# Reordering the steps ahead of the sort loop in a graph layer with residual and layer norm

## The chip, the cores and the metric

The kernel runs on one core of a Trainium2 chip. A core has a matrix engine (TensorE, in the profile PE, with its weight loads as PEld), a vector engine (VectorE, DVE), a scalar engine (ScalarE, ACT), a general engine (GpSimd, POOL) and a queue engine (SyncE, SP), which issues most of the transfers. Each runs its own list of instructions in order and waits for the others on semaphores. The metric is the device time of one execution in microseconds; the median of three runs is given.

## The reference

A node table x of 100,000 rows of 128 values, 50,000 edges with a source and a destination (ordered by destination), one weight matrix and a bias. Each edge sends the transformed row of its destination to its source; the sums are added to x and each row is normalised.

```python
row, col = (edge_index[0], edge_index[1])        # src, dst
messages = jnp.einsum('ei,oi->eo', x[col], W) + b
out = jax.ops.segment_sum(messages * agg_weight, row, num_segments=x.shape[0])
...
x = _layernorm(x + out, axis=-1)
```

## The kernel before, in words

The kernel first sorts the edges by source into a table and then walks over the nodes in 196 groups of 512. For every 4 groups (a period) there are 9 lists of up to 128 edges each; an edge's *bucket* is twice the number of its list, plus one if it lies in the last part of the list (its *tail*). Edges that a list can't hold spill into the next one.

**Decoding (DVE, lines 739 to 760).** The 50,000 sources lie in `src_rows` as 128 x 4 x 128. From them DVE makes the position in the span (`pos`), the list (`chunk`) and the bucket. The bucket's upper part (`e0`, up to 56 values) and lower part (`e1`, 16 values) are turned by PE (`turn_rows`, four 128x128 transposes each) so that edges lie along partitions, and DVE copies them to `hi_col` and `lo_col`. `hi_rows` goes to memory and comes back, spread over partitions, as `hi_row`.

**One-hots and totals (lines 764 to 770 and 539 to 545).** For each of 25 tile groups of 16 columns (2048 edges) DVE makes one-hots of both parts and PE adds up their products in one bank, 400 matmuls in all: the number of edges in each bucket.

**The rest of the way to the loop (lines 772 to 825).** DVE packs each edge into two words (`word1`, `word2`), copies sources and destinations as floats to `turn` (`chunk` is copied with the decoding), prepares constants (`ident_bf`, `not_earlier`, `part_half`), compares the first two row loads (`first_hots`), reads the totals (`counts`, `excess`), splits the bias in three parts (`b_parts` to `b3`), makes a running sum over the excess (`spill_row`) and from it the starting ranks (`origin`) and the largest list (`most_wide`). The excess goes through SP's queue into one row (`excess_row`), and the running sum back through it (`spilled`). PE turns the words and the float copies (lines 546 to 551), ScalarE copies them out (`s_cvt` counts, lines 1018 to 1021), and PE starts the loop when six copies are made.

**The sort loop (`count`/`place` on PE, `rank`/`spread` on DVE, `clip`/`second_word` on ScalarE).** For each tile group k PE counts ranks: products of one-hots, then a matmul that adds what came before (`carry`, for k = 0 from `origin`). DVE reads the ranks (`own`), and makes `slot`, `t_now` and `place_row`. Of the 16 columns of a group, 10 are placed by PE (`spread` makes the one-hots for it), and 6 by GpSimd, which scatters them to memory with indirect transfers (line 480), 141 in all. Work on k and the placing of k - 1 are interleaved by `lagging`.

**The overflow test.** In `rank(0)` DVE takes the largest list (turned by PE, `s_mxT`), sets the flag `over` and the factors `keep` and `dump` that make `place_row`. PE waits for the flag in group 1, since its ranks use the same bank.

**The main loop.** When all scatters have landed, SP loads the table back, DVE decodes it (36 columns first) and GpSimd gathers rows of x into `xg` by the table (line 517), a ring of 4 periods. Empty places in the table don't bring a row, so `xg` must hold no stray values at the start: GpSimd clears it (line 473) ahead of its first scatter. DVE, PE and ScalarE then make the sums, the projection and the norm of each group.

`after(...)` on DVE counts a semaphore up at an instruction's end and waits for it, so what follows doesn't overlap it:

```python
def after(ins):
    step_no[0] += 1
    ins.then_inc(s_bp, 1)
    dve.wait_ge(s_bp, step_no[0])
```

## Time and profile before

| | |
|---|---|
| median of three runs | 911.15 us (911.13 to 911.59) |
| the profiled execution | 912.28 us |
| its span, first to last instruction | 910.6 us |
| DVE busy | 853.0 us (94%) |
| PE busy / weight loads | 718.8 (79%) / 542.4 us (60%) |
| ScalarE busy | 650.4 us (71%) |
| GpSimd busy | 604.1 us (66%) |
| mean granted clock of PE | 0.931 |

The profile is one execution. Busy shares are averages over stages that differ: decoding and one-hots up to about 44 us, the sort loop up to about 247, the main loop from about 256 to the end. A row of a timeline gives the start, the length, the engine, the line and operation, output and inputs with sizes, how many such instructions were merged, and in brackets how long the engine was idle before it and who ended that. The granted clock is a share of TensorE's full 2.4 GHz: 1.00 or 0.50 (1.2 GHz).

### The profile page before, as it was taken

To read this page: it belongs to the slowest core of one execution; us is meant where nothing else is said; L and a number is where in the kernel's file an instruction comes from. 1 tells how busy PE (TensorE), PEld (TensorE's weight loads), DVE (VectorE), ACT (ScalarE), POOL (GpSimd) and SP (SyncE) were. 2 spreads that over 40 slices of the span, in tenths; PEclk is the share of its full clock that TensorE was granted. 3 is DMA by queue.
4 is the path that set the end of the run, shared out by engine and by line. 5 is a ranking of instruction groups with operands and counts; after the bars stand their busy time and mean duration, and the time that the engine had idled before them with its cause. 6 is when DMAs were issued, how large, how long until landed. Compare 5 with 4: busy or idle time off the path is not lost.

```text
span 910.6 us, 24246 instructions
## 1 busy us (share of the span) xinstructions
PE 718.8 (79%) x7748; PEld 542.4 (60%) x7773; DVE 853.0 (94%) x3868; ACT 650.4 (71%) x1683; POOL 604.1 (66%) x608
## 2 busy tenths in 40 slices
PE   3869999999638877777778877787878778787784
PEld 2835555555326656666666666676667667676664
DVE  7978999999658999999999999999999999999997
ACT  0147777777504778788778877777777887877788
POOL 3047777776657777777777777677777777777710
PEclk9969999999857999999999999989899999989988
DMA  2001111110043766676666667666666667666653
GB/s 73 2 26 37 39 41 39 43 37 26 16 134 108 209 212 214 220 215 215 206 212 212 208 211 212 205 209 211 208 220 207 205 214 215 208 214 202 217 176 124
DMA packets 81228, 141.20 MB, mean 155 GB/s; under 512 B 19552, under 2 KB 20588, under 8 KB 81100
## 3 DMA queue, kind: packets, MB, share of 16 engines
q1 hardware_dynamic: 62476, 110.55, 36.7%
q0 software_dynamic: 18624, 29.08, 13.3%
q8 instruction: 63, 1.03, 0.5%
q14 instruction: 65, 0.53, 0.2%
HBM read 87.64 MB, written 51.93 MB: 153 GB/s over the span
## 4 chain that ended last, share of the span: by engine, by line
DVE 61%; issue 7%; POOL 4%; ACT 1%; PE 1%; DMA 0%; ACTq 0%; DVEq 0%; POOLq 0%
DVE stats L994 16%; DVE h L988 10%; DVE sel L979 10%; DVE rest L977 8%; DVE xl L982 7%; DVE mv L1000 7%; POOL xg L517 3%; DVE rstd L1004 1%; ACT y L1087 1%; POOL place_scratch L480 1%; DVE shift L1008 1%; DVE now L965 1%; DMA xg<-in_x,now 0%; PE bank L719 0%; ACT aggT L1074 0%
## 5 line engine op out<-in xcount | busy, mean ns | idle before, releaser
L517 POOL DMA_INDIRECT xg<-in_x,now x441 | 449.0, 1018 | 172.9 <-issue 129.4
L1087 ACT ACTIVATE y<-h,shift,rstd 128x128 f32<-128x128 f32 x784 | 320.1, 479 | 0.1
L719 PE MATMUL bank<-wT,aggT 128*128 128x128 f32 x1568 | 241.5, 300 | 0.0
L719 PEld LDWEIGHTS bank<-wT,aggT 128*128 128x128 f32 x1568 | 202.6, 202 | 28.2 <-issue 11.9
L689 PE MATMUL bank<-sel,xg 128*128 128x308 bf16 (+11 forms) x685 | 171.1, 262 | 23.6 <-DVE xl L982 23.5
L480 POOL DMA_INDIRECT place_scratch<-word_col,place_row x141 | 142.1, 1008 | 55.6 <-issue 50.6
L691 PE MATMUL bank<-sel,rest 128*128 128x308 bf16 (+11 forms) x685 | 177.2, 262 | 0.0
L994 DVE BATCH_NORM_STATS2 stats<-h 128x6 f32<-128x128 f32 x784 | 169.5, 278 | 0.2
L693 PE MATMUL bank<-sel,xl 128*128 128x308 bf16 (+11 forms) x685 | 167.4, 261 | 0.0
L1081 ACT ACTIVATE std<-mv,eps 128x4 f32<-128x4 f32 x196 | 58.3, 298 | 132.7 <-DVE mv L1000 132.6
L988 DVE SCALAR_TENSOR_TENSOR h<-bank,aw,xt 128x512 f32<-128x512 f32 x196 | 145.6, 743 | 0.8 <-PE bank L719 0.4
L716 PE MATMUL bank<-b,deg 32*128 32x128 bf16 x784 | 39.1, 216 | 127.3 <-ACT aggT L1074 127.0
L1074 ACT COPY aggT<-bank 128x512 f32<-128x512 f32 x196 | 110.2, 562 | 30.9 <-PE bank L693 30.9
L979 DVE TENSOR_SCALAR sel<-iota_win,now 128x308 bf16<-128x308 f16 (+1 forms) x441 | 109.8, 296 | 0.0
L646 PE MATMUL bank<-oh_t,oh_s 128*128 128x441 bf16 x500 | 108.5, 355 | 1.6 <-ACT oh_s L1053 1.1
L716 PEld LDWEIGHTS bank<-b,deg 32*128 32x128 bf16 x784 | 24.4, 92 | 137.4 <-ACT aggT L1074 136.1
L977 DVE TENSOR_TENSOR rest<-xg 128x384 f32<-128x384 f32 x196 | 87.6, 447 | 12.3 <-DMA xg<-in_x,now 12.3
L689 PEld LDWEIGHTS bank<-sel,xg 128*128 128x128 bf16 x685 | 70.7, 103 | 35.3 <-issue 20.4
L1053 ACT ACTIVATE oh_s<-oh_s,ratio_col 128x128 bf16<-128x128 bf16 x250 | 83.9, 396 | 6.1 <-DVE oh_s L872 3.2
L982 DVE TENSOR_TENSOR xl<-rest 128x384 bf16<-128x384 f32 x196 | 88.1, 450 | 0.0
L874 DVE TENSOR_SCALAR oh_t<-iota_nb,t_now 128x441 bf16<-128x441 f16 x250 | 86.1, 344 | 0.0
L872 DVE TENSOR_SCALAR oh_s<-iota_nb,slot,word_col 128x128 bf16<-128x128 f16 x250 | 85.7, 343 | 0.0
(154 smaller groups left out, 927.1 us busy)
## 6 DMA issues: line engine op xcount, KB each, us to landing
xt<-in_x SPq DMA_DIRECT2D x195, 256.0 KB, 3.7
out<-y SPq DMA_DIRECT2D x195, 256.0 KB, 2.4
xg<-in_x,now POOLq DMA_INDIRECT x441
hi_row<-hi_scratch SPq DMA_DIRECT2D x50, 128.0 KB
place_scratch<-word_col,place_row POOLq DMA_INDIRECT x141
place_scratch<-scattered SPq DMA_DIRECT2D x1, 441.0 KB, 3.5
scattered<-place_scratch SPq DMA_DIRECT2D x1, 441.0 KB, 3.2
src_rows<-in_src SPq DMA_DIRECT2D x1, 192.0 KB
```

What stands on the lines that cost most here:

```text
L480: nc.gpsimd.indirect_dma_start(out=place_scratch, out_offset=bass.IndirectOffsetOnAxis(ap=place_row[:, k, i:i + 1], axis=0), in_=word_col[ ...
L517: nc.gpsimd.indirect_dma_start(out=xg[:, m, k], out_offset=None, in_=x, in_offset=bass.IndirectOffsetOnAxis(ap=now[:, m, k, 0:1], axis=0)) ...
L689: nc.tensor.matmul(AGG[q][:, nodes], top[:, ring, k, :, 1], sel[:, half, k, cols], start=(i == 0), stop=False, skip_group_check=True)
L691: nc.tensor.matmul(AGG[q][:, nodes], middle[:, half, k, :, 1], sel[:, half, k, cols], start=False, stop=False, skip_group_check=True)
L693: last = nc.tensor.matmul(AGG[q][:, nodes], xl[:, half, k], sel[:, half, k, cols], start=False, stop=(i == len(lists) - 1), skip_group_che ...
L719: last = nc.tensor.matmul(OUT[u % RO][:, nodes[j]], aggT[:, u % RO, nodes[j]], wT[:], start=False, stop=True, skip_group_check=True)
L977: V.tensor_tensor(rest[:, m % 2, lists], xg[:, m, lists], top[:, m, lists, :, 1], ALU.subtract).then_inc(s_upper, 1)
L979: V.tensor_scalar(sel[:, m % 2, k, 0:WIDTH[k]], iota_win[:, WIN[k]:WIN[k] + WIDTH[k]], now[:, m, k, 1:2], None, ALU.is_equal).then_inc(s_s ...
L982: V.tensor_tensor(xl[:, m % 2, lists], rest[:, m % 2, lists], middle[:, m % 2, lists, :, 1], ALU.subtract).then_inc(s_lower, 1)
L988: V.scalar_tensor_tensor(h[:, u].rearrange("p j d -> p (j d)"), OUT[u % RO][:], aw[:], xt[:, u].rearrange("p j d -> p (j d)"), ALU.mult, A ...
L994: V.bn_stats(stats[:, u, j], h[:, u, j]).then_inc(s_stats, 1)
L1087: nc.scalar.activation(y[:, u, j], h[:, u, j], ACT.Identity, bias=shift[:, u, j:j + 1], scale=rstd[:, u, j:j + 1]).then_inc(s_y, 1)
```

## The change

It touches the stretch between the first load and the sort loop, and one place in the loop's first group.

1. *Decoding.* The bucket is made in one piece: the whole position (`pos`, now with the upper bits) times 9, from which the upper part is one shift, and the lower part a mask, a shift-and-mask, a comparison and one two-input step that writes `turn[:, 2]` as floats. The upper part is copied for PE first, and PE waits for each part by itself. `hi_rows` has a semaphore of its own. `chunk` and its float copy move behind the totals.
2. *Totals.* `counts` and `excess` come right behind the one-hots, ahead of the words. The running sum comes ahead of `first_hots`.
3. *Transposes and copies.* PE and ScalarE take `word1` first, then `word2`, then `chunk`, sources, destinations; DVE's first ratio step waits for four copies, not six.
4. *Bias parts* come behind `most_wide`.
5. *Overflow test* in `rank(0)` comes behind `t_now`, ahead of `place_row`.
6. *xg* is cleared by ScalarE with one activation over 128 x 4608, ahead of its first copy, not by GpSimd.

```diff
@@ gpsimd
-            nc.gpsimd.memset(xg[:], 0.0).then_inc(s_clean, 1)
@@ tensor
-            pe.wait_ge(s_rows, 3)
+            pe.wait_ge(s_rows, 1)
             turn_rows(bank[1], turn[:, 1])
+            pe.wait_ge(s_rows, 2)
             turn_rows(bank[2], turn[:, 2])
...
-            pe.wait_ge(s_rows, 7)
+            pe.wait_ge(s_rows, 3)
+            turn_rows(bank[3], word1[:].bitcast(f32))
+            pe.wait_ge(s_rows, 4)
+            turn_rows(bank[2], word2[:].bitcast(f32))
             turn_rows(bank[0], turn[:, 0])
-            turn_rows(bank[3], word1[:].bitcast(f32))
-            turn_rows(bank[2], word2[:].bitcast(f32))
+            pe.wait_ge(s_rows, 6)
@@ vector, decoding
-            after(V.tensor_scalar(e1[:], src_rows[:], 2, P - 1, LSR, AND))
-            V.tensor_scalar(e2[:], src_rows[:], SPAN_N - GN, None, AND)
+            V.tensor_scalar(e1[:], src_rows[:], (1 << 18) - GN, None, AND)
+            after(V.tensor_scalar(e2[:], src_rows[:], 2, P - 1, LSR, AND))
             after(V.tensor_tensor(pos[:], e0[:], e1[:], OR))
-            after(V.tensor_tensor(e0[:], pos[:], e2[:], OR))
-            V.tensor_scalar(e2[:], src_rows[:], SPAN_BITS, None, LSR)
-            after(V.tensor_scalar(e0[:], e0[:], float(LISTS), None, ALU.mult))
-            V.tensor_scalar(e1[:], e0[:], SPAN_BITS, None, LSR)
-            after(V.tensor_scalar(e0[:], e0[:], SPAN_N - 1, None, AND))
-            after(V.scalar_tensor_tensor(chunk[:], e2[:], float(LISTS), e1[:], ALU.mult, ALU.add))
-            after(V.tensor_scalar(e0[:], e0[:], float(TAIL_FROM), None, ALU.is_ge))
-            after(V.scalar_tensor_tensor(bucket[:], chunk[:], 2.0, e0[:], ALU.mult, ALU.add))
-            V.tensor_scalar(e0[:], bucket[:], LO_BITS, None, LSR)
-            after(V.tensor_scalar(e1[:], bucket[:], LO - 1, None, AND))
-            V.tensor_copy(hi_rows[:], e0[:]).then_inc(s_rows, 1)
+            after(V.tensor_tensor(pos[:], pos[:], e2[:], OR))
+            after(V.tensor_scalar(bucket[:], pos[:], float(LISTS), None, ALU.mult))
+            after(V.tensor_scalar(e0[:], bucket[:], SPAN_BITS + LO_BITS - 1, None, LSR))
             V.tensor_copy(turn[:, 1], e0[:]).then_inc(s_rows, 1)
-            V.tensor_copy(turn[:, 2], e1[:]).then_inc(s_rows, 1)
-            V.tensor_copy(turn[:, 0], chunk[:]).then_inc(s_rows, 1)
+            V.tensor_scalar(e1[:], bucket[:], SPAN_N - 1, None, AND)
+            after(V.tensor_scalar(e2[:], bucket[:], SPAN_BITS, LO // 2 - 1, LSR, AND))
+            after(V.tensor_scalar(e1[:], e1[:], float(TAIL_FROM), None, ALU.is_ge))
+            V.scalar_tensor_tensor(turn[:, 2], e2[:], 2.0, e1[:], ALU.mult, ALU.add).then_inc(s_rows, 1)
+            V.tensor_copy(hi_rows[:], e0[:]).then_inc(s_hi_rows, 1)
+            dve.wait_ge(s_cols, 2)
+            V.tensor_copy(hi_col[:], bank[1][:]).then_inc(s_hilo, 1)
             dve.wait_ge(s_cols, 3)
-            V.tensor_copy(hi_col[:], bank[1][:]).then_inc(s_hilo, 1)
@@ scalar
+            act.wait_ge(s_made, 1)
+            nc.scalar.activation(xg[:].rearrange("p r k d -> p (r k) d"), ones[:].unsqueeze(1).broadcast_to([P, RX * LISTS, D]),
+                                 ACT.Copy, scale=0.0).then_inc(s_clean, 1)
```

What moves on DVE between the one-hots and the loop is shown by its order of instructions. DVE, from word2 on, before: the totals (`counts`, which wait for PE's 400 matmuls by `s_hist`) stand behind the copies, the constants and both row comparisons.

```order
L778 TENSOR_TENSOR word<-e 128x512 [waits s_bp]
L779 CAST turn<-src_rows 128x512
L780 CAST turn<-dst_rows 128x512
L781 CAST ident_bf<-ident 128x128
L782 TENSOR_SCALAR not_earlier<-later 128x512
L784 MEMSET spill_row 1x1
L786 TENSOR_SCALAR upper_half<-part 128x1
L787 TENSOR_TENSOR part_half<-part,upper_half 128x1 [waits s_bp]
L791 TENSOR_SCALAR oh_hiT<-hi_row,part_half 128x1024 [waits s_hrow0,s_bp]
L791 TENSOR_SCALAR oh_hiT<-hi_row,part_half 128x1024 [waits s_hrow1]
L797 TENSOR_TENSOR counts<-bank,guard 56x16 [waits s_hist]
L799 SCALAR_TENSOR_TENSOR excess<-counts 56x8 [waits s_bp]
```

The same engine in the changed kernel, right behind the last one-hot (L775 is the first step on `dst_rows`, L784 and L787 make `e0`, L785 makes `e1`):

```order
L775 TENSOR_SCALAR e<-dst_rows 128x512 [waits s_dst]
L776 TENSOR_SCALAR upper_half<-part 128x1
L778 TENSOR_TENSOR counts<-bank,guard 56x16 [waits s_hist]
L780 SCALAR_TENSOR_TENSOR excess<-counts 56x8 [waits s_bp]
L782 TENSOR_SCALAR word<-e 128x512
L783 TENSOR_SCALAR chunk<-bucket 128x512
L784 TENSOR_SCALAR e<-pos 128x512
L785 TENSOR_SCALAR e<-dst_rows 128x512
L786 CAST turn<-chunk 128x512 [waits s_bp]
L787 TENSOR_SCALAR e<-e 128x512
L788 TENSOR_TENSOR word<-e 128x512 [waits s_bp]
```

The totals have moved ahead of both words, so the words now stand behind the wait for PE.

PE in the changed kernel, from its last of the 400 matmuls (L542) to the first matmul of the sort loop (L597); before, all twenty transposes followed one wait for `s_rows`, with `chunk` first:

```order
L542 MATMUL bank4<-oh_lo,oh_hi 56x16 x15
L532 MATMUL bank3<-ident,word1 128x128 [waits s_rows]
L532 MATMUL bank3<-ident,word1 128x128 x3
L532 MATMUL bank2<-ident,word2 128x128 [waits s_rows]
L532 MATMUL bank2<-ident,word2 128x128 x3
L532 MATMUL bank0<-ident,turn 128x128 x4
L532 MATMUL bank6<-ident,turn 128x128 [waits s_rows]
L532 MATMUL bank6<-ident,turn 128x128 x3
L532 MATMUL bank1<-ident,turn 128x128 x4
L597 MATMUL bank6<-not_earlier,ident_bf 128x512 [waits s_hiT,s_cvt,s_zero]
```

The first four transposes can now start while DVE still makes word2; the loop's first matmul waits for the same six copies as before.

DVE in `rank(0)` of the changed kernel; before, L852 to L856 (the overflow test) stood ahead of `own`:

```order
L838 TENSOR_TENSOR own<-bank,oh_lo 128x256 [waits s_q,s_bp]
L842 TENSOR_REDUCE place_at<-own 128x16 [waits s_own]
L844 TENSOR_SCALAR beyond<-place_at 128x16 [waits s_place_at]
L846 SCALAR_TENSOR_TENSOR slot<-place_at,beyond 128x16 [waits s_beyond]
L848 SCALAR_TENSOR_TENSOR t_now<-beyond,t_col 128x16
L852 TENSOR_REDUCE most_all<-bank 128x1 [waits s_mxT]
L853 TENSOR_SCALAR over<-most_all 128x1 [waits s_bp]
L854 TENSOR_SCALAR keep<-most_all 128x1
L855 TENSOR_SCALAR most_all<-most_all 128x1
L856 TENSOR_SCALAR dump<-dump,most_all 128x400 [waits s_bp]
L859 SCALAR_TENSOR_TENSOR linear<-slot,t_now 128x16 [waits s_slot,s_bp]
L862 SCALAR_TENSOR_TENSOR place_row<-linear,keep,dump 128x16 [waits s_linear]
```

The five steps of the test now lie between the reading of the ranks and `place_row`.

## Rows read from the trace of the kernel before

**Rows 1.** The chain of waits at the sort's end: start us, length us, what.

```profile
247.20 8.37 issue
```

**Rows 2.** The page's groups: busy us, mean ns, idle us before and releaser.

```profile
L480 POOL DMA_INDIRECT place_scratch<-word_col,place_row x141 | 142.1, 1008 | 55.6 <-issue 50.6
```

**Rows 3.** Timeline of GpSimd, first scatter of tile groups 0, 1 and 2.

```profile
57.15 1.18 POOL L480 DMA_INDIRECT place_scratch<-word_col,place_row  x1 [7.66 <-issue]
...
67.12 0.96 POOL L480 DMA_INDIRECT place_scratch<-word_col,place_row  x1 [2.34 <-DVE place_row L864]
...
75.74 0.97 POOL L480 DMA_INDIRECT place_scratch<-word_col,place_row  x1 [0.89 <-DVE place_row L864]
```

**Rows 4.** Timeline of DVE from the totals to the first ranks.

```profile
40.20 0.16 DVE L797 TENSOR_TENSOR counts<-bank,guard 56x16 f32<-56x16 f32 x1
...
43.56 1.08 DVE L813 TENSOR_TENSOR_SCAN spill_row<-excess_row,zero_row 1x448 f32<-1x448 f32 x1
...
45.12 0.57 DVE L818 TENSOR_TENSOR ratio_col<-word_col,ratio_col 128x64 f32<-128x64 f32 x1
46.64 2.87 DVE L821 CAST origin<-spilled 56x8 bf16<-56x8 f32 x1 [0.95 <-DMA spilled<-spill_row]
...
49.78 0.28 DVE L825 TENSOR_SCALAR most_wide<-ones,most_hi 56x128 f32<-56x128 f32 x1
50.83 0.22 DVE L835 TENSOR_REDUCE most_all<-bank 128x1 f32<-128x56 f32 x1 [0.77 <-PE bank L624]
...
51.39 0.43 DVE L839 TENSOR_SCALAR dump<-dump,most_all 128x400 f32<-128x400 f32 x1
54.42 0.42 DVE L847 TENSOR_TENSOR own<-bank,oh_lo 128x256 bf16<-128x256 f32 x1 [2.60 <-PE bank L611]
```

**Rows 5.** Timeline of GpSimd ahead of its scatters.

```profile
43.98 1.08 POOL L470 CAST src_idx<-src_col 128x512 int32<-128x512 f32 x1 [35.72 <-ACT dst_col L1021]
...
45.55 3.93 POOL L473 MEMSET xg<- 128x4608 f32 x1
```

**Rows 6.** Timeline of PE: the totals, eight transposes, the origin matmul.

```profile
17.78 18.84 PE L542 MATMUL bank<-oh_lo,oh_hi 128*56 128x16 bf16 x400 [2.24 <-DVE oh_hi L770]
...
39.60 1.91 PE L533 MATMUL bank<-ident,word 128*128 128x128 f32 x8
...
49.59 0.32 PE L585 MATMUL bank<-origin,ident_bf 128*56 128x144 bf16 x1 [4.32 <-DVE origin L822]
```

**Rows 7.** Timeline of DVE during decoding.

```profile
7.38 0.69 DVE L744 TENSOR_TENSOR e<-pos,e 128x512 int32<-128x512 int32 x1
...
8.46 0.41 DVE L746 TENSOR_SCALAR e<-e 128x512 int32<-128x512 int32 x1
...
16.18 0.68 DVE L760 CAST lo_col<-bank 128x512 bf16<-128x512 f32 x1
```

**Rows 8.** Timeline of ScalarE, its first and its last copy before the loop.

```profile
9.27 0.27 ACT L1017 COPY wT<-bank 128x128 f32<-128x128 f32 x1 [7.17 <-PE bank L529]
...
43.25 0.58 ACT L1021 COPY dst_col<-bank 128x512 f32<-128x512 f32 x1 [0.27 <-PE bank L533]
```

**Rows 9.** Stretches: busy us of PE, PEld, DVE, ACT, POOL; granted clock, DMA share, GB/s.

```profile
36.70:44.00 7.30, 4.53 (x20) 4.22 (x22) 6.78 (x26) 3.00 (x5) 0.03 (x1) 1.00 0.00 0
46.70:49.60 2.90, 0.01 (x1) 0.01 (x1) 2.82 (x4) 0.00 (x0) 2.79 (x1) 0.60 0.54 180
49.60:54.40 4.80, 4.13 (x50) 2.49 (x52) 1.34 (x7) 2.61 (x6) 0.00 (x0) 0.50 0.02 4
```

**Rows 10.** Timeline of PE, the same work of tile groups 0 and 3.

```profile
51.20 1.01 PE L595 MATMUL bank<-not_earlier,ident_bf 128*128 128x512 bf16 x2
52.15 0.61 PE L601 MATMUL bank<-oh_hiT 64*128 64x128 bf16 x8
...
77.56 0.59 PE L595 MATMUL bank<-not_earlier,ident_bf 128*128 128x512 bf16 x2
78.08 0.40 PE L601 MATMUL bank<-oh_hiT 64*128 64x128 bf16 x8
```

More of the change, by code:

```diff
@@ L770, in _, with first_hots @@
                 V.tensor_tensor(oh_hi[:, k], pairs(hi_col, HI), digits(HI), ALU.is_equal).then_inc(s_ohk, 1)
+            def first_hots(k):
+                dve.wait_ge(s_hrow[k], 32)
+                V.tensor_scalar(oh_hiT[:, k], hi_row[:, k], part_half[:], None, ALU.is_equal).then_inc(s_hiT, 1)
             dve.wait_ge(s_dst, 48)
             V.tensor_scalar(e2[:], dst_rows[:], 4, 16, LSR, LSL)
-            after(V.tensor_scalar(e0[:], pos[:], 16, None, LSL))
-            V.tensor_scalar(word1[:], e2[:], FULL, None, OR)
-            V.tensor_scalar(e1[:], dst_rows[:], 15, 25, AND, LSL)
+            V.tensor_scalar(upper_half[:], part[:], 64.0, -64.0, ALU.is_ge, ALU.mult)
+            dve.wait_ge(s_hist, 1)
+            after(V.tensor_tensor(counts[:], SORT[0][0:HI, 0:LO], guard[:], ALU.add))
+            heads, tails = (counts[:].rearrange("h (c two) -> h c two", two=2)[:, :, i] for i in range(2))
+            V.scalar_tensor_tensor(excess[:], heads, -float(P), tails, ALU.add, ALU.add).then_inc(s_excess, 1)
+            V.tensor_scalar(word1[:], e2[:], FULL, None, OR).then_inc(s_rows, 1)
+            V.tensor_scalar(chunk[:], bucket[:], SPAN_BITS, None, LSR)
+            V.tensor_scalar(e0[:], pos[:], GN - 1, 16, AND, LSL)
+            after(V.tensor_scalar(e1[:], dst_rows[:], 15, 25, AND, LSL))
+            V.tensor_copy(turn[:, 0], chunk[:])
             after(V.tensor_scalar(e0[:], e0[:], FULL, None, OR))
```

61 lines of the change are left out of this document (27 added, 34 removed).

## The prediction

> **What bounds the kernel now.** I read first the chain of waits, to see which part of the program holds the end. For most of the span it is DVE in the main loop, which this change doesn't touch. Ahead of that loop the chain runs through GpSimd's scatters and then waits 8.37 us, while the last scatter lands, the table is read back and decoded [rows 1]. So the start of the main loop hangs on when the 141 scatters are through. The page's groups price them at 1.008 us each, idle time in front of them mostly GpSimd's own issuing [rows 2]. In GpSimd's timeline the scatters of tile group 0 start at 57.15 us, of group 1 at 67.12 and of group 2 at 75.74; only ahead of the last two does it wait for DVE's place_row (2.34 and 0.89 us idle, where 0.30 is its own pace), and the 129 scatters from 75.74 to 247.20 run without a gap that DVE makes [rows 1 to 3]. Whatever brings place_row of groups 0 to 2 forward by x brings the scatters' end, and the kernel's, forward by x. GpSimd's queue soaks up nothing.
>
> What releases group 0? DVE's timeline [rows 4], with GpSimd's [rows 5] and PE's [rows 6] beside it, gives the chain: sort totals read at 40.20, a trip through SP's queue, the running sum at 43.56, a second trip that lands at 46.64. Then a copy of 56 x 8 elements takes 2.87 us; the totals op of similar size took 0.16. Its end, 49.51, is the end of GpSimd's clearing of xg (45.55 + 3.93 = 49.48). PE has stood idle since 45.27 (49.59 less 4.32) for these origins. From its matmul at 49.59 it is 4.83 us of PE and ScalarE to DVE's reading of the ranks at 54.42. DVE is then busy without a gap until behind place_row of group 1.
>
> **The change, part by part.**
>
> *Shorter decoding.* Up to the second OR (7.38) DVE's steps are the same in number. There a one-input step on 128x512 takes 0.41; it puts the next start 0.35 later if nothing waits (8.11 to 8.46) and about 0.45 later if the next one waits; a two-input step takes 0.69 [rows 7]. From 8.11: multiply 0.45, shift 0.45, copy to turn 1 0.35, mask 0.35, shift-and-mask 0.45, compare 0.45, then the two-input step 0.69, which ends at 11.3. Four transposes are about 1.1 (eight took 1.91, [rows 6]), so turn 2 is through PE at 12.45; turn 1's went earlier and its copy to hi_col is over. lo_col 0.68 gives 13.2 for the first one-hot, where it was 16.9 (16.18 + 0.68): **3.7 us earlier**.
>
> *Totals right behind the one-hots.* PE's 400 matmuls ran 18.84 us without idle time and ended at 36.62, 1.2 us behind DVE's last one-hot: PE paces them. They now end at 32.9. DVE has then been waiting for about 0.9 us, with the two words queued behind it; that wait is new. Totals and excess take 0.35 and leave at 33.3, not 40.6.
>
> *The words.* From 33.3: four steps without a wait (word1, chunk, position, the float copy of chunk) at 0.35 and two with one at 0.45 are 2.3, word2 0.69: 36.3. Sixteen transposes follow (from 39.60 to 43.21, 3.6, [rows 6, 8]): 39.9. ScalarE's last copy is 0.58 [rows 8]: 40.5. From there to PE's readiness for the origins it was 1.44 us (43.83 to 45.27), so **PE is ready at 42.0**.
>
> *The origins.* The excess row landed within 3.0 us of its issue (40.6 to 43.56): 36.3 at the latest. Six steps stand between word2 and the running sum, 1.2 us in all, so it starts at 37.5, takes 1.08, and with the trip of 2.0 (44.64 to 46.64) lands at 40.6. Without the clearing the two origin steps need about 0.25: 40.85. That is earlier than 42.0. What was the late party has 1.1 us to spare, and PE's readiness, with the words, transposes and ScalarE's copies ahead of it, decides next. The origin matmul moves from 49.59 to 42.0, **7.6 us**.
>
> *From there to the ranks.* The 4.83 us ran at a granted clock of 0.50 (1.2 GHz), which fell while PE stood idle 4.32 us; it was 1.00 in 36.7 to 44, though PE was idle 2.8 of those 7.3 us [rows 9]. Now no gap after the one-hots is longer than about 1.5 us (between word1's transposes and word2's), so I take it that the clock stays. In this chain the pair of 128x512 matmuls and the eight behind it took 1.56 (51.20 to 52.76) and at 1.00 take 0.92 (77.56 to 78.48) [rows 10]: 0.64 gained. The ranks are read at 42.0 + 4.83 - 0.64 = 46.2 instead of 54.42, 8.2 us earlier.
>
> *The overflow test.* Its five steps (50.83 to 51.82, [rows 4]) lay in DVE's wait for the ranks and cost nothing. Now they stand between the ranks and place_row and cost **1.0**. PE's wait for the flag comes a group later and is met.
>
> *Bias parts.* Eleven steps, 3.05 us (40.48 to 43.53, just behind the totals), now follow most_wide, which ends at about 41.4. They end at 44.5, in the wait for the ranks (46.2). Cost 0; if the ranks came before 44.5 they would be the bound.
>
> *Clearing xg on ScalarE.* 4608 elements a partition are at most nine times its 512-element copy of 0.58, 5.2 us. ScalarE is idle from 2.1 to 9.27 [rows 8]; 7.3 at the latest. Cost 0. On SP's queue nothing new is passed: hi_rows goes out at 11.7 instead of 12.9, and its rows are first used at 38.6.
>
> *GpSimd's two casts stay* and start 0.15 behind ScalarE's last copy (43.98, [rows 5]), now 40.7, with the origin and totals steps. At 45.12 DVE's multiply of 64 columns took 0.57 beside the second cast. Bounds for what the casts cost: below 0, since the origins have 1.1 us to spare; above two casts of 0.6 in front of most_wide, 42.6, where PE wants it at 42.4 and its next wait has some slack: 0.4. I take 0, being nearest to the spare time.
> The Trainium skill (SBUF — State Buffer, the rule on the shared port pair) says that an instruction of VectorE or GpSimd that finds the pair taken is blocked for the whole of the other's; by it both casts would hold the origin steps, and the time would be 0.4 above mine. The 2.87 us copy agrees with it.
>
> Sum: -7.6 (origin matmul) - 0.64 (clock) + 1.0 (overflow test) = **-7.3 us** (rounded) for place_row of groups 0 and 1, and for the scatters. The profiled execution takes 912.28 (span 910.6 and 1.7 around it) and would take 905.0; the median of the runs lies 1.1 below it, 911.15, and would be **903.9**. About 0.2% (1.8 us) is what a measurement can tell from no change.
>
> **Rivals.**
> 1. *The clock still falls*, at 42 as at 49. For it: PE does little between 33 and 42; against: its gaps are short. The 0.64 is not gained, and with the casts' 0.4 the gain is 6.3 to 6.7: 904.5 to 904.9.
> The Trainium skill (TensorE: Matmul & The Clock Gate, on the warm-up) has the clock at half after an idle stretch; if the new, shorter gaps count as one, it gives 904.5 too. The trace agrees behind 49.6, where the clock read 0.50.
> 2. *Group 2 gains more.* GpSimd waited 0.6 longer than its pace for it [rows 3], while PE's count of that group ran partly at 1.2 GHz. If the clock is full there, up to 0.6 more: 903.3.
> 3. *The 2.87 us copy is not the clearing's doing* but that of the row loads, which moved 180 GB/s in just that stretch [rows 9]. Then the copy stays long; the origins come at 43.5, not 42.0, and the gain is 5.8: 905.4. Against it: the copy ends with the clearing to 0.03 us.
> 4. *Scatters get slower.* They take 0.96 alone and 1.10 or more where DVE holds them up; the mean is 1.008. If a new phase between the two queues made the mean 1.06, 141 x 0.05 = 7 us eat the gain: no change. Against it: the two run at different paces (about 8.0 and 7.4 us a group), so phases mix anyway.
> 5. *Slower.* DVE now waits for PE's 400 matmuls with everything else queued behind it. They take 47 ns each at a clock of 1.00. If the clock fell during the short decoding and they took twice that, 18.8 us more stand in the path: 11.5 slower, 922.7. It decides from 65 ns a matmul. Against it: PE's gaps ahead of them shrink.
>
> **How the numbers follow.** Forecast 0.5; rival 1 0.2; rival 2 0.12; rival 3 0.07; rival 4 0.05; rival 5 0.02; 0.04 for a main loop that falls differently in step with its transfers and moves by a microsecond either way. The predicted time is that of the forecast, 903.9. The range takes in rivals 1 to 3 and, beyond them, 0.5 each for the scatters' mean and the main loop below, 0.5 above: 902.3 to 905.9. Faster by over 0.2%: all but rivals 4 and 5 and a rest, 0.93; within 0.2% 0.04; slower 0.03.
>
> **What would show it.** First one-hot at 13.2; PE's 400 matmuls end at 32.9, totals right behind; word2 at 36.3; ScalarE's last copy to 40.5; origins at 40.9 with no DVE step of microseconds; the origin matmul at 42.0, held by PE's own transposes and no longer by DVE; PEclk 1.00 from 42 to 46; ranks at 46.2, overflow test behind them; first scatter near 50, the last ending at 239.9, unbroken from group 2 on. The clearing lies on ScalarE from 2 to at most 7.3. I am wrong if GpSimd waits for DVE after group 2, if the scatters' mean moves by more than 0.01 us, or if the main loop's length (655 us from the first gather) changes by more than 1.

## The result, and the profile after

| | before | after |
|---|---|---|
| median of four runs | 911.37 us (911.13 to 912.70) | 906.12 us (905.12 to 906.74) |
| ratio | | 0.9940 [0.9924, 0.9956] |
| the profiled execution, its span | 912.28, 910.6 us | 905.12, 903.4 us |
| first / last scatter issued | 57.15 / 247.20 | 49.12 / 239.15 |
| first gather of the main loop | 255.57 | 247.68 |
| first gather to the end of the span | 655.0 | 655.7 |

The kernel is 5.25 us faster; 7.3 was forecast, and 906.12 lies 0.2 above the range. Between the two profiled executions the gain is 7.16 us, close to the forecast, in part by luck: the front gained 8.0 and the main loop took 0.7 more. The profile before was of an execution 0.9 above the median, the profile after of the fastest of four, 1.0 below theirs: the whole miss lies in what these two profiles don't show. So the question is twofold: did each step of the front do what was said, and what differs from one execution to the next?

VectorE's timeline of the changed kernel (start us, length us, instruction, idle time before it):

```profile
33.00 0.17 DVE L778 TENSOR_TENSOR counts<-bank,guard 56x16 f32<-56x16 f32 x1 [0.83 <-PE bank L542]
...
35.54 0.69 DVE L788 TENSOR_TENSOR word<-e 128x512 int32<-128x512 int32 x1
...
37.50 1.08 DVE L797 TENSOR_TENSOR_SCAN spill_row<-excess_row,zero_row 1x448 f32<-1x448 f32 x1
...
40.56 0.48 DVE L807 CAST origin<-spilled 56x8 bf16<-56x8 f32 x1 [0.49 <-DMA spilled<-spill_row]
...
41.84 0.28 DVE L811 TENSOR_SCALAR most_wide<-ones,most_hi 56x128 f32<-56x128 f32 x1
...
44.73 0.35 DVE L823 SCALAR_TENSOR_TENSOR b<-b_parts,b_row,b_res 128x128 bf16<-128x128 bf16 x1
45.49 0.42 DVE L838 TENSOR_TENSOR own<-bank,oh_lo 128x256 bf16<-128x256 f32 x1 [0.40 <-PE bank L613]
46.79 0.21 DVE L852 TENSOR_REDUCE most_all<-bank 128x1 f32<-128x56 f32 x1
...
47.34 0.43 DVE L856 TENSOR_SCALAR dump<-dump,most_all 128x400 f32<-128x400 f32 x1
48.01 0.23 DVE L862 SCALAR_TENSOR_TENSOR place_row<-linear,keep,dump 128x16 int32<-128x16 f32 x1
```

Against [rows 4]: the totals are read at 33.00 instead of 40.20, the 2.87 us copy is down to 0.48, the bias parts end at 45.08, in front of `own`, and the overflow test stands behind it. PE beside it:

```profile
14.13 18.84 PE L542 MATMUL bank<-oh_lo,oh_hi 128*56 128x16 bf16 x400 [1.64 <-DVE oh_hi L768]
...
37.19 2.47 PE L532 MATMUL bank<-ident,turn 128*128 128x128 f32 x12
40.59 0.38 PE L597 MATMUL bank<-not_earlier,ident_bf 128*128 128x512 bf16 x1 [0.94 <-issue]
...
41.56 0.23 PE L587 MATMUL bank<-origin,ident_bf 128*56 128x144 bf16 x1
```

The origin matmul has no idle time of its own any more (4.32 us in [rows 6]); PE reaches it behind its own work. ScalarE clears `xg` long before anything needs it, and GpSimd's first scatters of the first three groups answer to [rows 3]:

```profile
2.10 4.04 ACT L1015 ACTIVATE xg<-ones 128x4608 f32<-128x4608 f32 x1
```

```profile
49.12 1.18 POOL L479 DMA_INDIRECT place_scratch<-word_col,place_row  x1 [7.52 <-issue]
...
59.08 0.97 POOL L479 DMA_INDIRECT place_scratch<-word_col,place_row  x1 [2.33 <-DVE place_row L862]
...
67.72 0.97 POOL L479 DMA_INDIRECT place_scratch<-word_col,place_row  x1 [1.02 <-DVE place_row L862]
```

All three are 8.0 us earlier. The page's group and the chain show that the sort keeps the gain whole: the mean scatter is unchanged against [rows 2], and the wait of 8.37 us at 247.20 [rows 1] begins 8.05 earlier.

```profile
L479 POOL DMA_INDIRECT place_scratch<-word_col,place_row x141 | 142.0, 1007 | 55.6 <-issue 50.4
```

```profile
239.15 8.53 issue
```

The first gather is 7.9 earlier, the end 7.2.

### The profile page after: what moved, and what is told of

It is laid out like the page before. It is cut to its first block, busy times and chain, and to the rows that moved or that the text cites. A ratio compares the mean times of both kernels' runs of the same rounds, so it can differ in the third digit from the quotient of the medians.

```text
span 903.4 us, 24243 instructions
## 1 busy us (share of the span) xinstructions
PE 724.3 (80%) x7748; PEld 546.4 (60%) x7773; DVE 849.8 (94%) x3865; ACT 654.6 (72%) x1684; POOL 599.4 (66%) x607
## 4 chain that ended last, share of the span: by engine, by line
DVE 61%; issue 6%; POOL 4%; ACT 1%; PE 1%; DMA 0%; ACTq 0%; DVEq 0%; POOLq 0%
DVE stats L992 16%; DVE h L986 11%; DVE sel L977 10%; DVE rest L975 8%; DVE xl L980 7%; DVE mv L998 7%; POOL xg L516 3%; DVE rstd L1002 1%; ACT y L1088 1%; POOL place_scratch L479 1%; DVE shift L1006 1%; DVE now L963 1%; PE bank L721 0%; DMA xg<-in_x,now 0%; ACT aggT L1075 0%
## 5 line engine op out<-in xcount | busy, mean ns | idle before, releaser
L721 PE MATMUL bank<-wT,aggT 128*128 128x128 f32 x1568 | 244.9, 303 | 0.0
L721 PEld LDWEIGHTS bank<-wT,aggT 128*128 128x128 f32 x1568 | 205.8, 205 | 28.8 <-issue 12.7
L479 POOL DMA_INDIRECT place_scratch<-word_col,place_row x141 | 142.0, 1007 | 55.6 <-issue 50.4
```

What stands on the lines that cost most here:

```text
L479: nc.gpsimd.indirect_dma_start(out=place_scratch, out_offset=bass.IndirectOffsetOnAxis(ap=place_row[:, k, i:i + 1], axis=0), in_=word_col[ ...
L721: last = nc.tensor.matmul(OUT[u % RO][:, nodes[j]], aggT[:, u % RO, nodes[j]], wT[:], start=False, stop=True, skip_group_check=True)
```

## The experiments

**What the later runs can and can't tell.** All later runs, on four chips, took 1242 to 1297 us, the kernel before among them (medians of its repeated runs 1280.3, 1260.7, 1255.8, 1255.5, and 1290.0 in a single execution), where the measurement above had 911. The kernel before, profiled there, gives on its page (chain of waits; groups with busy us, mean ns, idle us before and its cause):

```profile
PE 56%; issue 21%; DVE 8%; another core or an unknown queue 8%; ACT 5%; DMA 1%; ACTq 0%; POOL 0%; SPq 0%; DVEq 0%; POOLq 0%
...
L480 POOL DMA_INDIRECT place_scratch<-word_col,place_row x141 | 140.6, 997 | 159.0 <-DVE place_row L864 107.4
...
L716 PE MATMUL bank<-b,deg 32*128 32x128 bf16 x784 | 45.8, 244 | 117.6 <-issue 97.8
```

There PE holds the end, in good part with pauses that nothing in the profile explains ("issue"); before, it was DVE at 61%. GpSimd waits 107.4 us for `place_row` in the sort. But up to the first group's scatters the trace repeats that of the fast measurement: totals 40.20, the long copy 46.64 with 2.87 us, `own` 54.42, first scatter 57.15, each to 0.01. So the instants of the front are evidence from every run; from some 60 us on nothing compares with 911 (the first scatter of the second group, 67.12 there, is at 68.49), and a total shows only whether one kernel beats the other on such chips.

**The two kernels unchanged.**

> The kernel before, unchanged, profiled anew: the only comparison for the length of the main loop (from the first gather to the end of the span) that is of the same session as the changed kernel's. Its first gather was at 255.57 us, and the loop took 655.03 in the one profile at hand, whose own time was 1.1 above the median. Theory F (the front gains 8.0, the main loop gives 2 to 3 back): first gather 255.5, loop 653.5 to 654.5, total 911. Theory N (the loop is the same length in both, and the give-back is chance of few runs): loop within 0.5 of the changed kernel's.

Measured: 1259.75, ratio 0.9996 [0.9968, 1.0025]; first scatter 57.15. On the main loop it says nothing.

> The changed kernel once more, to see what its main loop costs in another execution. Theory F (the front gains 8.0 us, as the first profile shows, and the main loop gives some back): first gather again at 247.7, and a median of 905.5 to 906.5, so that gather to end is 1 to 2 us more than the 655 of before. Rival N (the loss was chance of one chip): median within 0.4 us of 903.3, that is 8.0 below before.

Measured: 1278.68, ratio 0.9977 [0.9942, 1.0011]; `own` 45.79, first scatter 49.42.

> The changed kernel, unchanged, profiled anew. F: first gather 247.7, loop 656 to 657, total 905.5 to 906.5. N: first gather 247.7, total within 0.5 of 903.3, the kernel before less 8.0. A session in which the kernel before itself takes far more than 911 us says nothing on either.

Measured: 1257.56, ratio 0.9989 [0.9951, 1.0028]. Neither F nor N is tested. What nobody had expected: `own` at 47.35 and the first scatter at 50.98, from the same instructions.

> The changed kernel a third time, for the speed of PE in the first group. So far two executions of it had the 512-column matmul of line 597 at 376 to 390 ns there and the first product on VectorE at 45.5 and 45.8, and two (one of them with the pause before the tables, which changes nothing ahead of it) had it at 586 to 634 ns and the product at 47.35, all at a recorded clock of 1.00. Theory G (whether PE is at full speed when the ranks begin differs from execution to execution, and is worth 1.6 us of the gain): one or the other again, product at 45.5 to 45.8 or at 47.3 to 47.4, nothing between. Rival H (it hangs on the chip or the session): then the value of that session, in all four kernels of this call.

Measured: 1271.52 in its one execution; `own` 45.81, first scatter 49.44.

> The changed kernel a fourth time. Theory G (full speed of PE at the start of the ranks is a matter of the execution): product at 45.5 to 45.8 with the 512-column matmul of line 597 at 376 to 390 ns, or at 47.35 with 586 to 634, or between them where PE changes speed midway (46.3 and 46.8 have been seen in variants). Should the kernel before run at 911 beside it, the total says whether the main loop gives time back: 905.5 to 906.5 if it does, 903.3 if not. At 1260 to 1290 it can't.

Measured: 1248.20, ratio 0.9947 [0.9917, 0.9977]; `own` 45.48, first scatter 49.11.

> The changed kernel a fifth time: one more look at PE's speed (product at 45.5, 45.8 or 47.35, where the four executions in these runs had 45.79, 47.35, 45.81, 45.48), and more executions for the ratio. Theory F+G (front gains 6.4 to 8.0 by PE's speed, and nothing beyond chance is lost behind it): 5 to 8 below the kernel before at 1260. If a session at this speed swallows the front's gain (PE's own feeding sets the pace from 60 us on): within 2 of it.

Measured: 1254.26, ratio 0.9979 [0.9951, 1.0008]; `own` 47.34, first scatter 50.97. PE's timeline in the fourth and in this one, first as it is at full speed:

```profile
40.37 0.59 PE L597 MATMUL bank<-not_earlier,ident_bf 128*128 128x512 bf16 x2 [0.72 <-issue]
...
42.91 0.59 PE L597 MATMUL bank<-not_earlier,ident_bf 128*128 128x512 bf16 x2
```

```profile
40.68 1.01 PE L597 MATMUL bank<-not_earlier,ident_bf 128*128 128x512 bf16 x2 [0.72 <-issue]
...
44.12 1.01 PE L597 MATMUL bank<-not_earlier,ident_bf 128*128 128x512 bf16 x2
```

The pair takes 0.59 or 1.01; of the two in [rows 10], the one of 0.59 stood where the granted clock read 1.00 and the one of 1.01 where it read 0.50. In these executions the record reads 1.00 in both cases (last section), so that the slow pair is PE at half speed is told from its length and not from the recorded clock. A smaller difference lies in the twelve transposes ahead: 2.45 and 2.47 in the two fastest executions, 2.77 in the other four, and ScalarE's last copy moves with them. Of six executions of the changed kernel, two had `own` at 45.5, two at 45.8, two at 47.35. Theory G holds: it differs from execution to execution, and H falls, since two kernels with the same front, run side by side on one chip, had 45.81 and 47.35 (the third execution here, and the moved reciprocal below). The kernel before had 54.42 both times: after its idle stretch of 4.32 us PE was at half speed in both.

Over the six the first scatter is at 49.12, 49.42, 50.98, 49.44, 49.11 and 50.97, mean 49.84: the front gains 6.2 to 8.0, **7.3 us in the mean**. That this is the forecast number is chance: it is a mixture of 8.0, 7.7 and 6.2. Of the totals, the fifth came out as the last of its expectations had it: 1254.26 is 1.3 below the kernel before beside it (1255.54).

**The clearing of xg.** Back on GpSimd, behind its two casts, in the changed kernel (the diff), and the reverse of it, alone, in the kernel before:

```diff
+            nc.gpsimd.memset(xg[:], 0.0).then_inc(s_clean, 1)
...
-            act.wait_ge(s_made, 1)
-            nc.scalar.activation(xg[:].rearrange("p r k d -> p (r k) d"), ones[:].unsqueeze(1).broadcast_to([P, RX * LISTS, D]),
-                                 ACT.Copy, scale=0.0).then_inc(s_clean, 1)
```

> The changed kernel with the clearing of xg back on GpSimd, behind its two casts. Theory P (GpSimd's clearing blocks DVE's small copies and two-input steps while it runs, 3.9 us): most_wide, at 41.84 in the changed kernel, is held until the clearing ends at about 45.5; the bias parts and the ranks follow; ranks at 48.9 instead of 45.5, first gather 3.4 later. Rival T (the long copy came from the row loads, 180 GB/s): no step is held, ranks at 45.5, total unchanged.

Measured: `own` 48.78, first scatter 52.41, 3.0 later than the executions of the changed kernel with PE alike (49.42 and 49.44); 1283.75, ratio 1.0007 [0.9972, 1.0043]. Timelines of VectorE and GpSimd:

```profile
40.60 0.17 DVE L809 CAST origin<-spilled 56x8 bf16<-56x8 f32 x1 [0.50 <-DMA spilled<-spill_row]
...
41.39 4.51 DVE L814 CAST b_parts<-b_bc 128x128 bf16<-128x128 f32 x1
```

```profile
41.89 3.93 POOL L474 MEMSET xg<- 128x4608 f32 x1
```

The clearing doesn't meet `most_wide`, as I had expected (that is done at 41.47), but another copy of VectorE's, and this one takes 4.51 us and ends 0.08 behind the clearing. Without the clearing it takes 0.21 in the profile above, and 0.63 in the first repeated execution, where it starts beside GpSimd's second cast as it does here. The origin copy, ahead of it, takes 0.17.

> The kernel before with the clearing of xg on ScalarE and nothing else. Theory P: the origin copy at 46.64 takes 0.2 us, not 2.87; PE's wait is 1.6 us, not 4.3, and its clock stays at 1.00; ranks about 3.3 earlier (51.1), first gather 3.3 earlier, total 908. Rival T: the copy stays at 2.9 us and the total at 911.

Measured: origin copy 0.17, `own` 51.81, first scatter 54.55, **2.6 earlier** than before; 1282.37, ratio 1.0011 [0.9976, 1.0046]. From its VectorE timeline:

```profile
46.65 0.17 DVE L819 CAST origin<-spilled 56x8 bf16<-56x8 f32 x1 [0.95 <-DMA spilled<-spill_row]
```

P holds twice. T falls: the row loads came at the same time as before (26 GB/s in 46 to 47 us in both, then 182 here and 191 before in 47 to 48), and the copy, at 46.82, was over before they had got going. Only the clearing can have held it until 49.51.

The rest of the expectation missed: the ranks are at 51.81, not 51.1. PE's timeline shows why:

```profile
46.94 0.26 PE L583 MATMUL bank<-origin,ident_bf 128*56 128x144 bf16 x1 [1.66 <-DVE origin L820]
...
48.60 1.01 PE L593 MATMUL bank<-not_earlier,ident_bf 128*128 128x512 bf16 x2
```

PE waited only 1.66 us, as said, and yet the granted clock read 0.52 in 47 to 48 us and the pair took 1.01. The half speed behind the origins does not need a wait of 4.32 us.

**Later decoding.** Nine more steps in front of it:

```diff
+            for _ in range(9):
+                after(V.tensor_scalar(e1[:], src_rows[:], 2, P - 1, LSR, AND))
```

> The changed kernel with nine idle steps of 0.46 us (4.1 us) on DVE ahead of the decoding: it does the same work, 4.1 us later. Theory S (the main loop's length depends on the instant at which it starts): first gather 4.1 later than the changed kernel, but the total later by another amount, apart by 0.5 us or more. Theory A (what is lost in the main loop comes with the new order of the steps ahead of it, not with the instant): total 4.1 later, 0.3 either way.

Measured: first one-hot 18.41, so the nine steps, 6.14 us in all, cost 5.16 net and not 4.1 (without them the decoding's own first two steps take 0.72 and 1.26 us, behind them 0.43 and 0.42); totals 38.16; origin copy 45.73; `own` 52.49; first scatter 56.12. PE was at half speed; against an execution of the changed kernel with the same (47.35, 50.98) every instant has moved by 5.14 to 5.16. The decoding is on the path one for one. Total 1283.35, ratio 1.0016 [0.9987, 1.0045]: S against A not told apart.

**Later totals.** The two steps that read the totals, put back behind the ten that pack and turn the words:

```diff
-            dve.wait_ge(s_hist, 1)
-            after(V.tensor_tensor(counts[:], SORT[0][0:HI, 0:LO], guard[:], ALU.add))
-            V.scalar_tensor_tensor(excess[:], heads, -float(P), tails, ALU.add, ALU.add).then_inc(s_excess, 1)
...
+            dve.wait_ge(s_hist, 1)
+            after(V.tensor_tensor(counts[:], SORT[0][0:HI, 0:LO], guard[:], ALU.add))
+            V.scalar_tensor_tensor(excess[:], heads, -float(P), tails, ALU.add, ALU.add).then_inc(s_excess, 1)
             after(V.memset(spill_row[:, 0:1], 0.0))
```

> The changed kernel with the two steps that read the totals put back behind the ten steps that pack and turn the words. By the chain as predicted (totals, running sum, landing of the spilled counts, origin, ranks): counts at some 37.8 instead of 33.0, the spilled counts landed some 4.5 later, the origin matmul on PE at 46.0 instead of 41.6, the product at 50 and the first scatter at 53.5 to 54: the gain of the front shrinks by 4.4. Rival: the four word copies of ScalarE and the first half of PE's work set the ranks anyway (PE reaches the origin matmul with no idle time now), then the product moves by less than 2.

Measured (one execution, 1275.04). VectorE's and PE's timelines:

```profile
36.30 0.16 DVE L792 TENSOR_TENSOR counts<-bank,guard 56x16 f32<-56x16 f32 x1
...
41.85 0.17 DVE L807 CAST origin<-spilled 56x8 bf16<-56x8 f32 x1
```

```profile
40.60 0.38 PE L597 MATMUL bank<-not_earlier,ident_bf 128*128 128x512 bf16 x1 [1.70 <-DVE oh_hiT L772]
...
43.63 1.01 PE L597 MATMUL bank<-not_earlier,ident_bf 128*128 128x512 bf16 x2
```

I had expected the ranks 4.4 later; the rival is right. The totals come 3.3 later, but the words come 1.06 earlier since nothing on DVE waits for PE's last totals, the spilled counts are there at 41.85 instead of 40.56, and PE's origin matmul stands at 42.14, where the executions at full speed had 41.54 to 41.88 (PE's 1.70 idle is now for the first compares of rows, behind the running sum on DVE). `own` at 46.84 is mostly PE's falling to half speed between the two rows. So reading the totals early, alone, is worth 0.3 to 0.6 us at the origin matmul, by one execution: once the decoding is shorter and the long copy gone, it and the words are nearly level.

**The product, the bias and the long reciprocal.** Three moves on DVE: the bias parts into its 9.6 us of waiting behind the sort, the overflow test ahead of `own`, the reciprocal of 448 columns from `k == 1` to `k == 3`.

```diff
-            after(V.tensor_copy(b_parts[:, 0], b_bc[:]))
...
-                if k == 1:
+                if k == 3:
                     after(V.reciprocal(ratio_col[:, early:], w1_col[:, early:]))
...
+                if k == 0:
+                    dve.wait_ge(s_mxT, 1)
+                    after(V.tensor_reduce(most_all[:], SORT[1][:, 0:HI], AX, ALU.max))
...
                 dve.wait_ge(s_q, k + 1)
...
+            after(V.tensor_copy(b_parts[:, 0], b_bc[:]))
...
             dve.wait_ge(s_place, C - SCATTERS)
             dve.wait_ge(s_scattered, 16)
```

> The changed kernel with three moves on VectorE: the bias parts (12 steps, 3.0 us) into its 9.6 us of waiting for the scattered words behind the sort, the overflow test ahead of the product that waits for the fourth count of PE, and the long reciprocal (2.9 us) from the second group to the fourth. If the way from the ranks to the scatters is what bounds the front: the product of the first group at 45.1 instead of 45.5, first place row 46.6 instead of 48.0, and the waits of GpSimd for the second and the third group (2.3 and 1.0 us) go; first gather 3 to 4.5 us earlier, total 2 to 4.5 below the changed kernel's. If PE or ScalarE is what they really wait for, the waits stay and only the 1.4 us of the first place row come: total 1 to 1.5 below.

Measured: 1256.05, ratio 0.9965 [0.9929, 1.0000]; timelines of VectorE and GpSimd:

```profile
45.80 0.42 DVE L833 TENSOR_TENSOR own<-bank,oh_lo 128x256 bf16<-128x256 f32 x1 [2.32 <-PE bank L613]
...
47.43 0.23 DVE L850 SCALAR_TENSOR_TENSOR place_row<-linear,keep,dump 128x16 int32<-128x16 f32 x1
```

```profile
48.53 1.18 POOL L479 DMA_INDIRECT place_scratch<-word_col,place_row  x1 [6.62 <-issue]
```

The test is hidden again: 2.73 us from `own` to the first scatter instead of 3.63. `own` itself doesn't move; DVE waits 2.32 for PE. GpSimd's wait for the second group stays too (3.75, where the changed kernel had 3.68 to 3.88 on these chips).

> The version with the bias parts, the overflow test and the long reciprocal moved, once more, for the same question: product at 45.8 with L597 at 376 to 390 ns, or at 47.3 with 586 to 634; first scatter 3.8 behind the product where the changed kernel has it 3.6 to 3.7 behind, less the 1.0 of the test: 2.7.

Measured: `own` 46.27, first scatter 49.00, 2.73 behind; 1265.10 in one execution. PE's first pair was at full speed, the next took 0.90: so "nothing between" is wrong, the change of speed can fall within the stretch.

> The changed kernel with the long reciprocal and its product (2.93 and 0.62 us) moved from the second group to the fourth, alone. If that is what GpSimd waits for ahead of the second group (2.33 us of waiting in the changed kernel): first scatter of the second group 2.3 earlier than 59.08 relative to the first one's, and no new wait. If PE is what VectorE waits for there: VectorE's waiting for PE grows by what the reciprocal leaves, and the second group starts less than 1 us earlier.

Measured: `own` 47.35; the second group's first scatter 11.51 behind the first one's, where the changed kernel with `own` at 47.35 had 11.31; total 1273.69 in one execution. DVE's waiting for PE ahead of the second `own` grew from 1.25 to 4.96 us. The gap that GpSimd sees isn't the reciprocal's on these chips; at 911 us, where the second group came 9.96 behind the first, it may be, which no run shows.

**PE's wait ahead of the ranks.** 24 small matmuls in PE's pause ahead of word2 and 12 ahead of the wait for ScalarE:

```diff
+            for _ in range(24):
+                nc.tensor.matmul(SORT[1][0:HI, 128:128 + LO], hi_of(0, 0), lo_of(0, 0), start=True, stop=True,
+                                 skip_group_check=True)
             pe.wait_ge(s_rows, 4)
...
+            for _ in range(12):
+                nc.tensor.matmul(SORT[1][0:HI, 128:128 + LO], hi_of(0, 0), lo_of(0, 0), start=True, stop=True,
+                                 skip_group_check=True)
             pe.wait_ge(s_zero, 1)
             pe.wait_ge(s_cvt, 6)
```

> The changed kernel with 24 small matmuls into an unused corner of a bank while PE waits for the second word (1.41 us idle) and 12 while it waits for ScalarE's last copy (0.94 us idle); the other instructions and their order are the same. Theory W (the half speed comes from PE's idling there): L597 at 376 to 390 ns at 40.6 to 40.9, product at 45.5 to 45.8, as in five of ten looks without them. If idling has nothing to do with it: half speed as often as without, product at 47.35 about every second time; one look can speak against W and only weakly for it.

Measured: 1252.03, ratio 0.9946 [0.9905, 0.9986]; `own` 45.79; PE:

```profile
34.80 1.29 PE L549 MATMUL bank<-oh_lo,oh_hi 128*56 128x16 bf16 x24
...
39.89 0.62 PE L558 MATMUL bank<-oh_lo,oh_hi 128*56 128x16 bf16 x12
40.68 0.59 PE L603 MATMUL bank<-not_earlier,ident_bf 128*128 128x512 bf16 x2 [0.17 <-issue]
```

> The changed kernel with the 36 small matmuls in PE's two pauses, a second look. Theory W (pauses cost PE its speed): L597 at 376 to 390 ns again, product at 45.8. If PE is at half speed here (586 to 634 ns, 47.35), the pauses aren't the cause. Total as the changed kernel's, at most 1.5 below it.

Measured: 1252.08, ratio 0.9968 [0.9935, 1.0000]; `own` 45.81, the pair 0.59. With the version below that has them too, PE began the ranks at full speed in three of three executions; without the small matmuls in eight of fourteen (all kernels taken together). Three in a row would come by chance once in five, so W is borne out, not shown. (The fourteen are all executions with the new front: six of the changed kernel and eight of its variants.)

> The version with the bias parts, the overflow test and the long reciprocal moved, with the same 36 small matmuls, and with PE starting the ranks behind ScalarE's fifth copy instead of its sixth (the sixth is needed only ahead of the first tables). If the last copy (ends 40.28) is what PE waits for in its 0.94 us: L597 at 40.0 instead of 40.6, product 0.3 to 0.5 earlier (45.2 to 45.4 at full speed), first scatter 47.9 to 48.2, that is 0.9 to 1.2 before the changed kernel's best and 9 before the kernel before's 57.15. If it waits for the one-hots of VectorE (end 39.28) or something else: the same instants as in the version without.

Its further edit is the diff below; the next version is the same without the small matmuls. Measured: 1251.62, ratio 0.9979 [0.9947, 1.0012]; L597's pair at 40.51, `own` 45.63, first scatter 48.36. The small matmuls themselves filled the pause to 40.5.

```diff
             pe.wait_ge(s_zero, 1)
-            pe.wait_ge(s_cvt, 6)
+            pe.wait_ge(s_cvt, 5)
...
+                    pe.wait_ge(s_cvt, 6)
                     pe.wait_ge(s_mx, 1)
```

> The version with the bias parts, the overflow test and the long reciprocal moved and with PE starting behind ScalarE's fifth copy, now without the small matmuls, which had filled the pause to 40.5 themselves. If PE waits for the copies: L597 at 40.0 to 40.3 (fifth copy out at 39.7 to 40.0), product at 45.1 to 45.3 at full speed, 46.8 at half; first scatter 2.7 behind it. Total 1 to 2.5 below the changed kernel's where PE's speed is the same. If something else holds PE: L597 at 40.6 or later.

Measured: 1249.08, ratio 0.9930 [0.9888, 0.9972]; PE:

```profile
39.83 1.01 PE L597 MATMUL bank<-not_earlier,ident_bf 128*128 128x512 bf16 x2
...
41.64 0.23 PE L587 MATMUL bank<-origin,ident_bf 128*56 128x144 bf16 x1
42.94 0.66 PE L597 MATMUL bank<-not_earlier,ident_bf 128*128 128x512 bf16 x2
```

The first pair starts 0.5 to 1.1 earlier and without idle time: ScalarE's last copy (40.00 to 40.58 there) is what PE waited for. It began at half speed though nothing held it just before, and recovered; `own` is at 45.59, and the first scatter at 48.32 is earlier than in any execution of the changed kernel. This is the best front found, and by its ratio it beats the kernel before; against the changed kernel beside it (0.9979 [0.9951, 1.0008]) the intervals overlap, so a shorter total isn't shown. The earlier first scatter is: the four executions with the test ahead of `own` have 48.32 to 49.00, the six of the changed kernel 49.11 or later. As `own` isn't earlier than the changed kernel's best (45.48), the gain is that of the hidden test.

**A pause behind the sort.** Nine fills on DVE ahead of the tables' reading:

```diff
+            for _ in range(9):
+                after(V.memset(emp[:], 0))
             V.tensor_tensor(i1, TABLES[0][:, 0:NB].bitcast(i32), other1, OR).then_inc(s_dec1, 1)
```

> The changed kernel with some 4 us (9 small fills in a row) on VectorE between the end of the sort and the reading of the tables; everything before it and after it is the same instructions. Theory S (the length of the main loop hangs on the instant at which it starts): total not at +4 but apart from it by over 0.5; first gather +4. Theory A (the loss comes with the new order of the front, in whatever way): total +4.0, give or take 0.3.

Measured: 1262.30, ratio 1.0033 [0.9999, 1.0067], 4.7 above the changed kernel beside it (1257.56, medians), with intervals of 4 us each way: it neither supports S nor excludes it.

## Why the prediction missed, step by step

- *Shorter decoding*, first one-hot at 13.2: 13.25. Right, and one for one on the path (*Later decoding*).
- *Totals*, PE's matmuls to 32.9, read behind them: 32.97 and 33.00. Right. Of what the step is worth alone nothing was said; it is 0.3 to 0.6 us.
- *The words*, word2 done at 36.3, transposes to 39.9, last copy to 40.5, PE at the origins at 42.0: 36.23, 39.66, 40.28, 41.56. Right in kind; with the slower transposes 41.88. That PE would wait for ScalarE's last copy was right too (the last version of *PE's wait*).
- *The origins*, ready at 40.85 with 1.1 to spare: last origin step 40.96 to 41.11, ahead of PE. The long copy was the clearing's (both runs on it), not the loads': rival 3 falls. GpSimd's casts held VectorE too, by less: in the profiled execution they end at 41.03 and 41.60, and the origin copy (0.48) and the step on `head_end` (0.57) end 0.01 behind them; the step between (40.96 to 41.11) took 0.15. Nothing of it lay on the path. The rule of the Trainium skill (SBUF — State Buffer, on the shared port pair) agrees with both: the held steps, of 2.87, 4.51, 0.48 and 0.57 us, all end within 0.1 of GpSimd's instruction.
- *The clock stays*, -0.64: this step was taken as settled and isn't. PE did stay at full speed in the profiled execution (`own` at 45.49 for 46.2), but in two of six it did not, and then `own` is at 47.35. Rival 1 had the mechanism, with a chance of 0.2, and priced it at 0.64. That fits its own stretch: from the origin matmul to `own` it is 3.92 us in the first repeated execution (41.87 to 45.79) and 4.61 in the fifth (42.73 to 47.34). But PE was slow ahead of the origin matmul as well, 0.86 there, which makes 1.55, and 1.86 against the fastest executions, whose transposes were shorter too. Both slow executions are of the later chips: whether this befell any of the unprofiled ones at 906 isn't known.
- *The overflow test*, 1.0: `own` to place_row is 2.52, it was 1.63 (56.05 less 54.42): 0.89, and moving it ahead of `own` gave that back. Bias parts and clearing: 0, right.
- *Sum of the front*, -7.3 (its terms add up to 7.24): -8.0 in the profiled execution. The origin matmul came 8.03 earlier for 7.6, the ranks 3.93 behind it for 4.19, and the test cost 0.89 for 1.0. In the mean of six executions it is 7.3. The mean scatter moved by 0.001 us: rival 4 falls; PE's 400 matmuls took 18.84 again: rival 5 falls.
- *From the front to the median*: this is the **step that failed**. The prediction had the profiled execution at 905.0 and the median 1.1 below it, since it lay so before, and took the main loop's length as fixed within 0.5, with a chance of 0.04 for more. The profiled execution took 905.12, but the median lies 1.0 above it. Even the 905.0 came out by two errors that cancel: 0.7 more gained in the front, 0.7 lost in the loop (655.7 for 655.0). From the median of the kernel before and a front of -7.3, 904.1 was due (911.37 less 7.3); 906.12 is 2.0 more. None of the prediction's three signs of being wrong shows in the profiled pair (the idle time ahead of the scatters is 55.6 us in both, their mean moved by 0.001, the loop by 0.7): they were signs for a profile, and the miss lies in executions without one.
- *What the missing 2.0 is*, worked out, not read, for no other execution at 906 was profiled. If the three unprofiled runs after (905.72, 906.53, 906.74) had the profiled one's front, their loops took 656.3 to 657.3 us. The four runs before, less the front of their profile, give 653.9 to 654.3 for three and 655.5 for the one at 912.70; then the loop is longer by 0.9 to 3.5 us. But if the three had the slow front (1.9 later), their loops took 654.5 to 655.5, and need not be longer at all. Either would make the whole miss, and no run separates them. In the profiled pair the loop is 0.7 longer; over 300 us of it, from 44 us behind the first gather on, the granted clock is 0.93 against 0.95 and PE is busy 239.7 us instead of 235.3. A lower clock isn't what sets the three slower runs apart, though: their mean granted clock is 0.932 to 0.940, that of the fastest 0.926.

What stays open is whether the loop or the front took the missing time, and if the loop, why: its start instant, PE's clock, or chance among four runs. On the chips of the later runs the ratios of the changed kernel were 0.9977, 0.9989, 0.9947 and 0.9979, some 1.4 to 6.7 us of 1250 to 1280, whole front gain or part of it.

## What to carry to other kernels

When a wait at half the clock goes, take PE's speed in the new order as open, price at both speeds all of PE's work in the new stretch, not only what followed the old wait, and put about half the weight on each (here PE began at full speed in 8 of 14 executions; a first pair that started right behind the transposes, without a pause, was slow in its one execution). Set a forecast against several executions: a profile before and one after that lie 1 us off their medians, on opposite sides, hide or invent 2 us, as much as the whole range allowed on its upper side. And a long VectorE step that ends with a long GpSimd fill is the fill's: move the fill to an idle engine, but look which VectorE step it would find otherwise.

## What the hardware showed that was not expected

The granted clock of the records doesn't always show PE's speed at that instant. Windows of the fifth execution of the changed kernel (us, busy by engine, granted clock, DMA share, GB/s), whose pairs of 128x512 matmuls took 1.01 at 40.68 and 44.12:

```profile
40.00:46.00 6.00, 5.30 (x56) 2.81 (x56) 3.93 (x17) 2.40 (x6) 1.21 (x2) 1.00 0.29 90
46.00:54.00 8.00, 6.09 (x60) 2.61 (x62) 6.42 (x29) 3.91 (x11) 2.42 (x3) 1.00 0.00 0
```

It reads 1.00 throughout. In the fourth, whose pair took 0.60 at 45.78, the same stretches read:

```profile
40.00:46.00 6.00, 4.71 (x90) 3.08 (x91) 4.67 (x19) 2.99 (x8) 1.19 (x2) 1.00 0.31 90
46.00:54.00 8.00, 5.60 (x51) 2.31 (x49) 7.79 (x32) 4.46 (x12) 3.98 (x4) 0.79 0.01 0
```

That both are the same speed levels is inferred from the lengths: the other forms of the fifth agree (sixteen matmuls of line 571 in 0.71 us at 42.17, as at 54.24 in the kernel before, where the clock read 0.50, and 0.47 at full speed). So the length of one matmul form is the better witness. The second surprise is that the same program had a median of 906 us in one measurement and of 1248 to 1279 in all others, with the kernel before in step (911, and 1256 to 1290). From some 60 us on PE pauses there with no cause in the profile, while VectorE's instants in the kernel before, ahead of that, agree to 0.02 us. Why PE pauses wasn't found.
